# The weighted sum of four branches: GpSimd's share of it moved to VectorE, two terms to a unit

## The reference

```
# layer 0: a low-rank adapter picked by language_ids
h = relu(x @ W1[lang] + b1[lang]);  y = x + h @ W2[lang] + b2[lang]
x = x + layernorm(y) * gamma[lang] + beta[lang]
# layer 1: two of four experts picked by type, three shared branches, and a gate per sequence
expert_out = out_a * wa + out_b * wb          # out_e = relu(x @ wi[e]) @ wo[e]
gi = concat(expert_out[:, 0], s0[:, 0], s1[:, 0], s2[:, 0])
g = softmax(relu(gi @ gate_w1) @ gate_w2)     # four weights per sequence
out = expert_out*g[:,0] + s0*g[:,1] + s1*g[:,2] + s2*g[:,3]
x = x + out
```

## Time and profile before

| what | us |
|---|---|
| median of 3 runs | 89.88 (89.76 to 90.19) |
| the profiled execution, whole | 90.16 |
| its span, first to last instruction | 88.3 |
| busy in the span: PE, DVE, ACT, POOL | 80.3, 60.9, 51.9, 39.1 |
| mean granted TensorE clock | 0.974 of full speed |

### The profile page before, as it was taken

The page is one execution under the profiler, slowest core; times in us unless marked ns, Lnnn a source line. Parts: engine busy times, 40 slices in busy tenths (PEclk is TensorE's granted clock), DMA queues, the critical chain, the costliest instruction groups (busy, mean ns, idle before and its releaser), DMA issues.

```text
span 88.3 us, 1638 instructions
## 1 busy us (share of the span) xinstructions
PE 80.3 (91%) x458; PEld 67.0 (76%) x458; DVE 60.9 (69%) x178; ACT 51.9 (59%) x119; POOL 39.1 (44%) x76
## 2 busy tenths in 40 slices
PE   4995895999999999999999999999999998978850
PEld 1251863588788888899888999988999997967720
DVE  5248556889999754555547377675598599799870
ACT  6002980369976979988696655555666452564310
POOL 5942239100698399998644300000000089792600
PEclk9999999579999999999999999999999999999997
DMA  0543813997999355740000000000000000002204
GB/s 1 142 126 73 224 22 53 252 281 223 349 334 276 119 179 147 183 145 0 0 0 7 0 0 0 0 0 0 0 7 0 0 4 4 0 0 59 64 3 119
DMA packets 12029, 7.50 MB, mean 85 GB/s; under 512 B 2389, under 2 KB 10867, under 8 KB 12019
## 3 DMA queue, kind: packets, MB, share of 16 engines
q1 hardware_dynamic: 10928, 7.03, 28.7%
q10 hardware_dynamic: 962, 0.33, 1.4%
q0 software_dynamic: 128, 0.02, 0.2%
HBM read 5.80 MB, written 0.52 MB: 72 GB/s over the span
## 4 chain that ended last, share of the span: by engine, by line
PE 66%; DVE 17%; DMA 5%; issue 3%; ACT 2%; SPq 2%; DVEq 1%
PE bank L944 10%; PE bank L924 10%; PE bank L925 10%; PE bank L928 9%; PE bank L942 9%; PE bank L941 9%; DVE comb L786 7%; DVE hl L734 4%; PE bank L872 3%; DMA lang_p<-in_itok_B_dram 3%; PE bank L891 2%; DMA W1s<-in_L_cond_W_dram 2%; SPq L341 1%; PE bank L901 1%; PE bank L969 1%
## 5 line engine op out<-in xcount | busy, mean ns | idle before, releaser
L734 DVE SCALAR_TENSOR_TENSOR hl<-bank,hh 128x256 fp32r<-128x256 f32 (+2 forms) x60 | 31.5, 525 | 15.2 <-ACT hh L521 14.5
L521 ACT ACTIVATE hh<-bank 128x256 fp32r<-128x256 f32 (+2 forms) x60 | 28.2, 469 | 16.7 <-PE bank L928 16.0
L444 POOL TENSOR_TENSOR wl<-w_raw,wh 128x512 fp32r<-128x512 f32 x17 | 21.6, 1294 | 8.3 <-ACT wh L514 8.3
L944 PE MATMUL bank<-hl,wh 128*128 128x256 f32 (+2 forms) x60 | 20.1, 335 | 1.1 <-DVE hl L734 1.0
L941 PE MATMUL bank<-hh,wh 128*128 128x256 f32 (+2 forms) x60 | 19.8, 329 | 0.0
L942 PE MATMUL bank<-hh,wl 128*128 128x256 f32 (+2 forms) x60 | 19.6, 326 | 0.0
L514 ACT ACTIVATE wh<-w_raw 128x512 fp32r<-128x512 f32 x18 | 11.3, 628 | 5.3 <-issue 5.3
L944 PEld LDWEIGHTS bank<-hl,wh 128*128 128x128 f32 x60 | 11.3, 189 | 2.8 <-DVE hl L734 1.9
L924 PE MATMUL bank<-x1hl,wh 128*128 128x256 f32 (+1 forms) x36 | 12.5, 346 | 0.0
L942 PEld LDWEIGHTS bank<-hh,wl 128*128 128x128 f32 x60 | 11.4, 190 | 0.8
L941 PEld LDWEIGHTS bank<-hh,wh 128*128 128x128 f32 x60 | 11.4, 190 | 0.8
(11 more groups left out here) (108 smaller groups left out, 110.0 us busy)
## 6 DMA issues: line engine op xcount, KB each, us to landing
w_raw<-in_L_cond_expert_wi_dram SPq DMA_DIRECT2D x6, 256.0 KB, 5.4
w_raw<-in_L_cond_expert_wo_dram SPq DMA_DIRECT2D x6, 256.0 KB, 5.8
xs<-x1hl SPq DMA_DIRECT2D x8, 128.0 KB, 3.0
w_raw<-in_L_cond_share_wi_dram SPq DMA_DIRECT2D x3, 256.0 KB, 3.7
w_raw<-in_L_cond_share_wo_dram SPq DMA_DIRECT2D x3, 256.0 KB, 4.2
out_dram<-o_sb SPq DMA_DIRECT2D x4, 128.0 KB, 1.9
x_in<-in_x_dram SPq DMA_DIRECT2D x1, 256.0 KB, 3.1
x_in<-in_x_dram ACTq DMA_DIRECT2D x1, 256.0 KB, 4.4
```

Source lines behind the costliest of these rows:

```text
L444: nc.gpsimd.tensor_tensor(wl[:, k, w, :], w_raw[:, k, buf(w), :], wh[:, k, w, :].bitcast(f32), ALU.subtract).then_inc(s_wl[w], 1)
L521: nc.scalar.activation(packed(hh[:, u % NBUF, :], r), packed(h_ps[u % NBUF][:, :], r), ACT.Relu).then_inc(s_hh, 1)
L734: nc.vector.scalar_tensor_tensor(out=packed(hl[:, u % NBUF, :], r), in0=packed(h_ps[u % NBUF][:, :], r), scalar=0.0, in1=packed(hh[:, u % ...
L944: nc.tensor.matmul(dst, wh[:, 1, w, chunk], lo, start=False, stop=(c == FC - 1)).then_inc(s_mm2, 1)
```

## The change

GpSimd's 14 terms are given to DVE as `mixture_term`s. The table of terms is now two to a unit: sequences 0 to 3, one after the other, after units 47 to 54; terms 0, 1 and 2 of sequences 4 to 7 after units 53 and 54, 55 and 56, 58 and 59. GpSimd's code for the mixture, its tiles and its semaphore go, and PE waits for DVE's count alone.

```diff
-    BY_POOL = (0, 1)
-
-    MIXTURE_AT = [[(4 + i, i % G, 2 + i // G) for i in range(2 * G)],
-                  [(4, 0, HB), (5, 0, HB + 1), (6, 1, HB), (7, 1, HB + 1), (9, 2, HB), (10, 2, HB + 1)]]
+
+    MIXTURE_AT = [[(4 + i // 2, i % G, i // G) for i in range(HB * G)],
+                  [(at + j // 2, i, HB + j) for i, at in enumerate((4, 6, 9)) for j in range(HB)]]
...
-            pool.wait_ge(s_g, 1)
-            for b in BY_POOL:
-                link(nc.gpsimd.tensor_tensor(prod[:, :, :], mix[:, :, seq(b)],
-                                             g[:, 0, b, :].unsqueeze(2).to_broadcast([P, G, S]), ALU.mult))
-                link(nc.gpsimd.tensor_tensor(prod2[:, :, :], prod[:, 0:2, :], prod[:, 2:4, :], ALU.add))
-                link(nc.gpsimd.tensor_tensor(prod1[:, 0, :], prod2[:, 0, :], prod2[:, 1, :], ALU.add))
-                nc.gpsimd.tensor_tensor(comb[:, b, :], prod1[:, 0, :], x1T[:, seq(b)], ALU.add).then_inc(s_part, 1)
...
             for b in range(HB, B):
-                if b == B - PAIR:
-                    dve.wait_ge(s_part, len(BY_POOL) + 1)
                 mixture_term(G - 1, b)
...
-                    if b in BY_POOL:
-                        pe.wait_ge(s_part, BY_POOL.index(b) + 1)
-                    else:
-                        pe.wait_ge(s_comb, b + 1 - len(BY_POOL))
+                    pe.wait_ge(s_comb, b + 1)
```

More of the change, by code:

```diff
@@ L186, in conditional_residual_mlps @@
         g = sb("g", [P, NH, HB, G])
-        prod = sb("prod", [P, G, S])
-        prod2 = sb("prod2", [P, G // 2, S])
-        prod1 = sb("prod1", [P, PAIR, S])
         comb = sb("comb", [P, B, S])
@@ L266, in conditional_residual_mlps @@
         s_store = sem("s_store")
-        s_part = sem("s_part")
         s_dve = sem("s_dve")
```

## The result

The changed kernel has a median of 90.85 us (4 runs, 90.66 to 91.20), the kernel before 89.82 (4 runs, 89.76 to 90.19). The ratio is 1.011, with a 95% interval of 1.0067 to 1.0153. Forecast were 90.77 us, in a range of 89.8 to 91.3.

A forecast was written before the change was run, and what follows sets the result against it. DVE was taken as the bound behind the gate's weights: -2.65 + 3.12 + 0.96 = +1.43 us up to unit 57, then 2.08 in place of 2.62, in all +0.89: 89.88 + 0.89 = 90.77 us, range 89.8 to 91.3.

The forecast's parts named there:

- DVE is the bound between units 47 and 59: Behind the gate's weights DVE sets the pace: 1.07 us per unit before the change, where PE could do 0.72.
- The stopping goes: With GpSimd silent, DVE's terms are no longer held up: 2.65 us less before unit 57, 0.44 behind unit 57.
- Twelve more terms: From unit 47 to the start of unit 57 DVE gets 12 more terms at 0.26 us each: +3.12 us.
- Eight dependent pairs: After units 47 to 54 the second term waits for the first, 0.12 us more per pair: +0.96 us (0 to 1.1).
- Unit 57 at 82.86: Start of unit 57 after the first stretch's sum of +1.43 us; it was 81.43 before.
- From there to the last terms: From unit 57's start to the last four terms: 2.08 us in place of 2.62, so these start at 84.94.
- The wait of 0.28 for ACT goes: DVE's idle 0.28 us ahead of unit 58 vanishes: data there at 83.02, DVE free at 83.20.
- The sum, +0.89: The last terms start at 84.94 in place of 84.05, shifting the tail and the total by 0.89 us.
- The rival of the clock: PE pauses more and drops to 1.2 GHz, 1.35 us per unit over 12 units: 4.4 us more, 95.2; chance 0.02.
- a granted clock under 1.00 before 84 us: One of the signs listed beforehand that would show the prediction wrong: PE's clock lowered before 84 us.

The follow-up runs named there:

- no_pairs: Changed kernel with the 16 terms of sequences 0 to 3 reordered, so that a unit's two terms never depend on each other; 89.89 us against 89.91 before.
- changed_again: The changed kernel unaltered, run again for more executions; 90.77 us against 90.12 for the kernel before, ratio 1.0078.
- pool_last_two: Against the kernel before: DVE takes sequences 0 and 1 without dependent pairs, GpSimd keeps terms of 6 and 7; four of six executions: median 91.1 us against 89.99.
- pool_silent: Kernel before with GpSimd's 14 mixture terms left uncomputed, DVE's instructions the same; 87.50 us against 89.91, ratio 0.9739.
- pool_dummy: Changed kernel with GpSimd's 13 mixture instructions put back, writing to a tile nobody reads; 95.42 us against 89.91 for the kernel before, ratio 1.0602.

## Why the prediction was right, by its steps
- *DVE is the bound between units 47 and 59.* Right: the reordering on DVE alone took 0.99 us off the stretch, and a halved clock of PE for 3 us added nothing to it (14.27 against 14.26 us).
- *The stopping goes, -2.65 before unit 57 and 0.44 behind.* Right. All 28 terms are at 0.35 us; silencing GpSimd in the kernel before gave 3.0 us back to DVE.
- *Twelve more terms, +3.12.* Right: a pair of independent terms is 0.60 us, 0.34 + 0.26.
- *Eight dependent pairs, +0.96.* Right, and the heart of it: 0.38 us in every pair, and 0.99 us less in the stretch of `no_pairs`. That the two medians differ by just 0.96 us (90.85 and 89.89) is luck in the last digits: they come from different chips. The page of the Trainium skill that stood against this entry (VectorE: DVE Perf Modes, "The DRAIN you can't avoid") says that the semaphore costs nothing extra, of a measurement on eight tensor copies. For these terms it doesn't hold: independent ones start 0.26 us apart, dependent ones 0.38. The prediction left out that the same section lets a next operation that is not held start earlier; the independent terms agree with that, by 0.08 us.
- *Unit 57 at 82.86.* 12.17 us behind unit 47 were forecast, 82.54 - 70.35 = 12.19 measured. *From there to the last terms* 2.08, measured 84.62 - 82.54 = 2.08. *The wait of 0.28 for ACT goes:* it did.
- *The sum, +0.89.* Measured +0.91 in the stretch. The spans differ by 0.6 only because the early part differs by chance. In the profiled execution of before the clock was low in two slices between 15 and 20 us, in that of the change it wasn't, and unit 47 came 0.34 us earlier. `changed_again` has such a dip, and its unit 47 is at 70.67. The clock rows of the change and of `changed_again`:

```profile
PEclk9999999999999999999999999999999999759995
```
```profile
PEclk9999999669999999999999999999999999999996
```

  All twelve profiles divide in this way. The six without the early dip have unit 47 at 70.21 to 70.38, five of the six with it at 70.67 to 70.77, and the sixth, `pool_last_two`, at 71.06. It is probably also why the executions of the kernel before fall in two groups some 0.4 us apart, about 89.8 with a mean clock of 0.986 and more, and about 90.2 with 0.981 and less; for executions without a profile the place of the dip is not on record.
- *The rival of the clock* was wrongly argued, though the time is right: one of the prediction's own signs of being wrong, a granted clock under 1.00 before 84 us, did come. I held a busy share of 2.28 of 3.00 at clock 1.00 for proof that it stays. The change lengthened one single wait, PE's for the gate's products, from 0.34 to 1.06 us, and behind it the clock fell in one of two profiles. The wait grew because DVE, slower by the pairs, came to unit 51 late: 74.28 - 70.35 = 3.93 us behind unit 47, where it had been 73.85 - 70.69 = 3.16. The products themselves stand no further behind unit 51 than before, 0.98 us against 1.04. I priced a unit at the low clock at 1.35 us; in the profile a matmul comes every 0.21 us, six to a unit, 1.28. It cost nothing because DVE needs more than that for each unit of that stretch: 1.59 us for unit 52 with the gate's weights, and 1.51 us each for units 53 and 54, which hold four terms. Units 55 and 56 take DVE about 0.86 us each; had the fall reached them, PE's 1.28 us would be the longer time. The rival's 4.4 us counted the low clock over 12 units, and it lasted about 3.3 us, under three units of PE. That the fall ended in time was luck.

## What to carry to other kernels
Moving work from GpSimd to an engine that is already the bound can be free, if the helper's instructions stopped that engine before: count the stopped time of the receiving engine (duration beyond the undisturbed one) before calling the helper a help. Here it differed by place: GpSimd's instructions for sequences 0 and 1 stopped DVE for 1.2 us and saved it 2.1, those for 6 and 7 stopped it for 1.9 and saved 1.6. These are prices in the order of the kernel before; with another order the latter stopped DVE for 1.7. And on a saturated engine the order counts as much as the number: interleave chains, so that no instruction waits for the one before it, and put a request to another engine ahead of independent work.

## What the runs showed of the hardware that I had not expected
- A DVE instruction that waits for its predecessor's result starts 0.03 to 0.04 us after its end, an independent one 0.08 us before it: 0.38 against 0.26 us for a 128x128 term.
- The stop bears on terms with both tensors in SBUF; `hidden_low`, which reads one from PSUM, stayed at 0.41 to 0.43 us beside GpSimd in every kernel. That GpSimd's float32 instructions stop a float32 operation of this kind at all is shown by `pool_silent` and `pool_dummy`. The prediction asked whether the block that the Trainium skill names for two-port modes covers such an operation. The same page says so in another section (Advanced Engine Details and Errata, "GPSIMD Details"): GpSimd also conflicts with VectorE instructions that have two inputs in SBUF. The traces agree.
- After single PE waits of 1.1 us (the changed kernel), 1.6 us (`pool_last_two`) and 2.0 us (`pool_dummy`) the granted clock went to 0.50 in the profile; after one of 1.1 us in another execution of the changed kernel it did not.
